# A two-layer transformer on one core: products with the values for four heads at once, in every second step

## The reference

```
h = layernorm(x) * (1 + ca) + sa;  x = x + ga * attention(h)
h = layernorm(x) * (1 + cb) + sb;  x = x + gb * experts(h)
```

```
scores = q @ k.T * 8 ** -0.5;  p = exp(scores - max);  out = (p @ v) / sum(p)
```

## Time and profile before

| | us |
|---|---|
| median of three runs | 1835.53 |
| lowest and highest | 1829.68 and 1887.89 |
| the profiled execution | 1856.04 |
| its span, first to last instruction | 1854.3 |
| first to last scores of the dense attention | 78.4 to 531.8 |
| first to last scores of the causal attention | 818.0 to 1447.2 |

### The profile page before, as it was taken

One profiled execution on the slowest core, in us unless ns is written; L12 is line 12 of the kernel. 1 busy time (PEld: TensorE's weight loads), 2 busy tenths in 40 slices (PEclk: granted clock), 3 DMA queues, 4 the chain that ended last, 5 costly groups with the idle time before them and its releaser, 6 DMA issues.

```text
span 1854.3 us, 40002 instructions
## 1 busy us (share of the span) xinstructions
PE 1575.2 (85%) x12803; PEld 808.0 (44%) x12803; DVE 1279.0 (69%) x3451; ACT 1192.9 (64%) x2134; POOL 885.1 (48%) x1677
## 2 busy tenths in 40 slices
PE   5799999999967999789999999999998409988870
PEld 3333444444433444234444444444444307777650
DVE  6565777776747888836767676666767537776657
ACT  3776777877756989635555655655645607888760
POOL 6243554545511333424443447657465654555445
PEclk9898999999988999879999998999989659999995
DMA  5221222121208920121212122222222322222218
GB/s 152 80 38 24 45 37 36 41 41 36 46 14 334 386 109 1 46 44 41 49 41 47 36 44 69 57 47 65 46 52 42 122 98 70 77 72 75 67 55 264
DMA packets 238478, 141.21 MB, mean 76 GB/s; under 512 B 184162, under 2 KB 210658, under 8 KB 237252
## 3 DMA queue, kind: packets, MB, share of 16 engines
q1 hardware_dynamic: 227072, 119.72, 24.4%
q0 software_dynamic: 8640, 17.97, 3.0%
q10 hardware_dynamic: 2564, 0.97, 0.2%
HBM read 37.67 MB, written 58.98 MB: 52 GB/s over the span
## 4 chain that ended last, share of the span: by engine, by line
PE 41%; DVE 13%; issue 6%; DVEq 2%; ACT 2%; POOL 2%; POOLq 1%; DMA 1%; SPq 0%; ACTq 0%; another core or an unknown queue 0%
PE OP L2136 8%; PE OP L2001 5%; PE M L2099 4%; PE SP L1981 4%; DVE mx L1326 4%; PE SP L2296 4%; PE M L2074 2%; PE SP L2116 2%; PE M L2095 2%; PE M L2090 2%; DVE pt L1617 2%; POOL h_dram L492 2%; PE OP L2311 2%; PE OP L2148 1%; PE M L1991 1%
## 5 line engine op out<-in xcount | busy, mean ns | idle before, releaser
L863 ACT ACTIVATE pt<-SP 128x768 f32<-128x768 f32 x256 | 207.4, 810 | 257.8 <-PE SP L2116 245.7
L1326 DVE TENSOR_REDUCE mx<-M 128x2 f32<-128x512 f32 (+1 forms) x384 | 257.9, 683 | 111.6 <-PE M L2099 103.7
L531 POOL TENSOR_SCALAR_AFFINE_SELECT pt<-pt 128x256 f32<-128x256 f32 x512 | 200.0, 415 | 273.4 <-ACT pt L863 271.7
L750 ACT ACTIVATE pt<-SP 128x1024 f32<-128x1024 f32 x256 | 255.8, 1020 | 80.4 <-PE SP L1871 80.3
L562 POOL DMA_INDIRECT y_dram<-hT,dest x142 | 138.3, 974 | 146.3 <-DVE hT L1623 123.7
L961 ACT ACTIVATE pt<-SP,b 128x256 f16<-128x256 f32 x284 | 137.4, 484 | 88.9 <-PE SP L2296 86.6
L1890 PE MATMUL OP<-pt,vs 128*32 128x256 f32 x1408 | 189.0, 391 | 0.0
L1617 DVE TENSOR_TENSOR pt<-vs,pt 128x256 f16<-128x256 f32 x284 | 117.1, 423 | 70.2 <-ACT vs L962 49.4
L2136 PE MATMUL OP<-pt,vs 128*32 128x128 f32 (+1 forms) x1408 | 156.0, 345 | 5.1 <-POOL pt L531 5.1
L492 POOL DMA_INDIRECT h_dram<-hT,slot x128 | 130.5, 1020 | 57.7 <-issue 31.6
L2296 PE MATMUL SP<-ksT,shared 128*128 128x256 f16 x852 | 130.0, 276 | 31.3 <-DVE ksT L1592 28.3
(11 more groups left out here) (325 smaller groups left out, 3362.2 us busy)
## 6 DMA issues: line engine op xcount, KB each, us to landing
h_dram<-shared SPq DMA_DIRECT2D x8, 4488.0 KB, 33.5
hT<-h_dram SPq DMA_DIRECT2D x71, 132.0 KB
rows<-g_dram SPq DMA_DIRECT2D x4, 2048.0 KB, 7.1
pt<-y_dram SPq DMA_DIRECT2D x32, 256.0 KB, 3.5
x_sb<-in_x SPq DMA_DIRECT2D x8, 512.0 KB, 8.8
pt<-in_w SPq DMA_DIRECT2D x4, 1024.0 KB
out<-x_sb SPq DMA_DIRECT2D x16, 256.0 KB, 3.0
shared<-st SPq DMA_TRANSPOSE x144, 2.4
```

The source lines that it names most:

```text
L531: last = pool.affine_select(out=diag, in_=diag, compare_op=ALU.is_ge, fill=0.0, base=0, pattern=[[0, 2], [1, P]], channel_multiplier=-1)
L750: act.activation(pt[:, u % 4], SP[u % 2][:], ACT.Exp, scale=SCALE).then_inc(s["exp"], 1)
L863: act.activation(pt[:, u % 4, :, 0:384], SP[u % 2][:, :, 0:384], ACT.Exp, scale=SCALE).then_inc(s["exp"], 1)
L1326: dve.tensor_reduce(to, M[:, k % 2, :].rearrange("p (j k) -> p j k", j=4 if k < 4 else 2), AX.X, ALU.max).then_inc(s["mred"], 1)
```

## The change

In both attentions `values` takes a group of four heads, j, in place of a step of two: for each half of the keys it issues the matmuls of all four heads, on the four column groups of the array, and then adds 2 to `pv`. It is called only in steps with odd u, for the group that ended in the step two before the last (u = 1: group 3 of the batch before; u = 3, 5, 7: groups 0, 1, 2), and waits for both steps' exponentials (dense) or selections (causal). The number of matmuls and their sizes stay.

The other work is moved. Dense: the projection of the first half of the tokens goes to step 0, that of the second half to step 2 (both were in step 1); `turn` goes from step 5 to 6. Causal: `values` now comes last in its step, behind the projections, `tail_wo`, all three fills, `router` and `back`; `enter` and `turn3` go from step 6 to 7. No other engine's list changes.

```diff
-                def values(b, u):
-
-                    if u == 0:
+                def values(b, j):
+
+                    if j == 0:
                         pe.wait_ge(s["vs"], b + 1)
-                    pe.wait_ge(s["exp"], CH * b + u + 1)
-                    if b and u % 4 == 0:
-                        pe.wait_ge(s["o"], 2 * b + u // 4 - 1)
-                        if u:
+                    pe.wait_ge(s["exp"], CH * b + 2 * j + 2)
+                    if b and j % 2 == 0:
+                        pe.wait_ge(s["o"], 2 * b + j // 2 - 1)
+                        if j:
                             pe.wait_ge(s["wr"], b)
-                    j = u // 2
+                    c = (j % 2) * T
                     for k in range(TT):
-                        for i in range(2):
-                            g = 2 * (u % 2) + i
-                            c = (j % 2) * T
+                        for g in range(HG):
                             last = pe.matmul(OP[32 * g:32 * g + 32, j // 2, c:c + T],
                                              vsd[b % 3][:, k, HG * j + g, :],
-                                             pt[:, u % 4, i, k * T:k * T + T],
+                                             pt[:, 2 * (j % 2) + g // 2, g % 2, k * T:k * T + T],
                                              start=(k == 0), stop=(k == TT - 1),
                                              skip_group_check=True, tile_position=(0, 32 * g))
-                    last.then_inc(s["pv"], 1)
+                    last.then_inc(s["pv"], 2)
...
                         score(b, u)
                         if b == 0 and u == 2:
                             pe.wait_ge(gl_in, 1)
-                        if CH * b + u >= 2:
-                            values((CH * b + u - 2) // CH, (u - 2) % CH)
-                        if u == 1 and b + 3 < B:
-                            for t in range(TT):
-                                project(b + 3, t)
+                        if u % 2 and CH * b + u >= 3:
+                            values((CH * b + u - 3) // CH, (u - 3) % CH // 2)
+                        if u in (0, 2) and b + 3 < B:
+                            project(b + 3, u // 2)
                         if u == 4 and b:
                             tail_wo(b - 1)
-                        if u == 5 and b >= 3:
+                        if u == 6 and b >= 3:
                             turn(b - 3)
                         if u == 7 and b >= 3:
                             router(b - 3)
-                values(B - 1, CH - 2)
-                values(B - 1, CH - 1)
+                values(B - 1, NJ - 1)
```

In `causal`, `values` is changed in the same way (it waits for `sel`), and the order is:

```diff
                         score(b, u)
-                        if FILLS[u] and b + 1 < B:
-                            fill(b + 1, done)
-                            done += 1
-                        if CH * b + u >= 2:
-                            values((CH * b + u - 2) // CH, (u - 2) % CH)
                         if u == 0 and b + 2 < B:
                             project(b + 2, 0)
                             project(b + 2, 1)
                         if u == 4 and b:
                             tail_wo(b - 1)
-                        for _ in range(FILLS[u] - 1):
+                        for _ in range(FILLS[u]):
                             if b + 1 < B:
                                 if done == 2 and b in WARM:
                                     keep_warm(b, u + 1, WARM[b])
...
                         if u == 5 and b >= 6:
                             router(b - 6)
                             back(b - 6)
-                        if u == 6:
+                        if u == 7:
                             if b + 3 < B:
                                 enter(b + 3)
                             if b >= 5:
                                 turn3(b - 5)
+                        if u % 2 and CH * b + u >= 3:
+                            values((CH * b + u - 3) // CH, (u - 3) % CH // 2)
                         if u == 7 and b - 1 in CHOSEN:
                             positions(CHOSEN.index(b - 1))
-                values(B - 1, CH - 2)
-                values(B - 1, CH - 1)
+                values(B - 1, NJ - 1)
```

More of the change, by code:

```diff
@@ L2119, in score, with values @@
                     last.then_inc(s["score"], 1)
-                def values(b, u):
-                    if u == 0:
+                def values(b, j):
+                    if j == 0:
                         pe.wait_ge(s["vs"], b + 1)
[L2125 to L2128, removed]
+                    pe.wait_ge(s["sel"], CH * b + 2 * j + 2)
+                    if b and j % 2 == 0:
+                        pe.wait_ge(s["o"], 2 * b + j // 2 - 1)
+                        if j:
                             pe.wait_ge(s["wr"], b)
-                    j = u // 2
+                    c = (j % 2) * T
                     for k in range(TT):
                         q0 = P if k else 0
-                        for i in range(2):
-                            g = 2 * (u % 2) + i
-                            c = (j % 2) * T
+                        for g in range(HG):
                             last = pe.matmul(OP[32 * g:32 * g + 32, j // 2, c + q0:c + T],
                                              vs3[b % 3][:, k, HG * j + g, :],
-                                             pt[:, u % 4, i, k * T:k * T + T - q0],
+                                             pt[:, 2 * (j % 2) + g // 2, g % 2, k * T:k * T + T - q0],
                                              start=(k == 0), stop=(k == TT - 1),
                                              skip_group_check=True, tile_position=(0, 32 * g))
-                    last.then_inc(s["pv"], 1)
+                    last.then_inc(s["pv"], 2)
                 def tail_wo(b):
```

## The result

The changed kernel takes 2000.74 us (median of 6, 1980.28 to 2015.32), the kernel before 1841.47 beside it (6 runs, 1829.68 to 1890.31): a ratio of 1.082, 95% interval 1.0766 to 1.0874. Every ratio here is taken over a kernel's runs without the few that fell into a slower state, so it is not the quotient of the two medians. The changed kernel is 161 us slower than predicted and outside the predicted range. The profiled execution took 2002.92 us, with a span of 2001.2.

The account below looks back on a forecast made before the run. It took TensorE and a loop through ScalarE to bind dense together, with VectorE's maxima holding up causal blocks. Dense -4, causal -18 and clock +25 gave +3 us; against the 1835.5 median it said 1840, range 1790 to 1905.

Parts of the forecast that it names:

- The clock: Causal block steps: half clock in about every second batch, some 5 us long, ended by the next four-head group; costs 25 us.
- rival C: Both attentions: half-clock stretches in every second batch last 14 us or more; 1895 us, slower, chance 0.15.
- The waits that I walked: Dense batch: scores 5 wait for exp 3, TensorE idles nearly 2 us there, and `turn` still finds z not made.
- rival E: Whole kernel: TensorE is the only bound and the walked waits mostly vanish; 1725 us, dense batch 11 us, chance 0.12.
- The saving of 0.15 us a batch: Dense loop through `high`: the stretch after the router shortens from 2.62 to 2.48 us; 4 us over 28 batches.
- The sum to 14.41: Dense batch: durations along the loop through ScalarE add up to exactly 14.41 us, read as that loop binding beside TensorE.
- Four column groups: `values`: four heads run side by side, so a group costs what two did, 0.99 us dense and 0.77 causal.
- rival D: `values`: four column groups don't run side by side, never more than two; 1897 us, slower, chance 0.10.
- The estimate of 1.15 us: Dense `values` group: cost by the skill's 3.07x for four row tiles, which would make the sum some 20 us more.
- Causal walk: Causal batch walked step by step with its waits: 18.55 us against 19.19, saving 18 us over 28 batches.
- The batch of 18.5: Causal: the batch length expected where the clock is full, against 19.19 us before.
- Rival B: Both attentions: no new half-clock stretches, so only the savings of 22 to 24 us remain; 1812 us, chance 0.18.

Follow-up runs that it names:

- e1: Changed kernel plus matmuls that nobody reads, 12 per dense batch and 9 per causal batch: 1902.22 us, ratio 1.0265 to the kernel before.
- e10: Changed kernel with each four-head group's products issued as two pairs, one after the other: 2029.64 us, ratio 1.0995 to the kernel before.
- e7: Kernel before with four heads at once in dense alone, old places, plus 8 and 8 unread matmuls ahead of `tail_wo` and `turn`: 1784.15 us, ratio 0.9879.
- e12: Kernel before with four heads at once in dense alone, old places, plus 4 and 4 unread matmuls ahead of `tail_wo` and `turn`: 1825.57 us, ratio 0.9884.
- e5: Changed kernel's new places in both attentions, but products of two heads in every step as in the kernel before: 1920.12 us, ratio 1.0358.
- e13: Changed kernel with TensorE waiting for a group's first pair of heads before issuing the second: 2044.24 us, ratio 1.1298 to the kernel before.
- e6: Kernel before with four heads at once in dense alone, everything else in its old place: 1785.8 us, ratio 0.9872.
- e4: Changed kernel with four heads at once kept in both attentions, but all other work back in its old place: 1947.95 us, ratio 1.0555.
- e9: Kernel before plus 9 unread 512-column matmuls per causal batch in steps 2 to 4: 1847.76 us, ratio 1.022.
- e8: Kernel before with four heads at once in causal alone, old places, plus three unread 512-column matmuls in steps 2 and 4: 1825.22 us, ratio 1.009.

## Why the prediction was wrong

**The clock, the step that failed.** I put it at 28 batches x 0.5 x 5 us x 0.35 = 25 us in causal, and at nothing in dense. The place was right: the clock falls in the block steps of the causal batch (1116.0, in step 3, between the seventh block and the eighth). How often was wrong by a factor of two: every batch, not every second. How long was wrong by three: 491 us over 31 stretches is 15.8 each, as the two that I had in front of me were 13.7 and 17.1. I set those rows aside for an argument, that the dense group that follows would bring the clock back; nothing in the trace stood for it, and the group at 1118.40 shows the opposite. The price was near: with 19.0 us for a full-clock batch (e1), (737 - 31 x 19.0) / 491 = 0.30 us lost per us at half, and single batches of the change (24.0 us, 17 of them at half) give 0.29. So the term was 31 x 15.8 x 0.30 = 147 us in causal, not 25; the stage is longer by only 124, because the kernel before had lost some 11 us at half too and its full-clock batches are longer (19.2). This is rival C with its own length taken in every batch, which I gave 0.15 and priced at half.

**Dense.** The waits that I walked came: TensorE idles 1.8 to 2.0 us before scores 5 ("nearly 2"), and rival E's 11 us did not come. The saving of 0.15 us a batch was too small. The change's shortest batches, with 3 us at half clock in them, take 13.4 and 13.6, and e10's one batch without any takes 13.4, against 13.9 on average before (most 13.7 to 14.4); in the old places (e7, e12) it is 13.0. The sum to 14.41 could not show that ScalarE's loop binds: it adds up the distances from one place in the batch to the same place in the next, which gives the batch by whatever path. This error put the forecast too high; what put it too low is that I wrote that idle time down as free. It is what the clock answered to: 215 us at half, and 22 us more for the stage instead of 4 less. In the trace the falls in dense come with the longest waits (252.4 behind 1.79 us, 450.4 with 1.96), and where filler took the waits away the falls went too (e7: 3 stretches, 14 us). Those in causal do not: TensorE was busy 6.47 of the 6.9 us that ended at 1116.0. The Trainium skill, page "TensorE: Matmul & The Clock Gate", section "Part 1: The HAM clock gate", ties a fall to idle gaps; dense agrees in kind, causal is nearer to what the same page says under "A second HAM failure mode: psum-queue depth-cycling", that short idle times between groups of matmuls can make the clock swing too. No run here tests that against the thin work of the blocks themselves.

**Four column groups.** Right, and rival D is out: sixteen matmuls take 1.00 us (301.53 to 302.53 after), starting in fours within 20 ns, and 0.79 in causal. The timeline after:

```profile
301.53 1.07 PE L1888 MATMUL OP<-pt,shared 128*32 128x256 f32 x16
302.53 0.39 PE L1871 MATMUL SP<-shared 32*128 32x256 f16 x4
```

The estimate of 1.15 us that I drew from the Trainium skill's four row tiles does not carry over to four column tiles.

**Causal walk.** Its waits came: 0.25 and 0.61 us for the blocks, 0.86 for `turn3` (0.8 predicted), this one at half clock. The batch of 18.5 was never seen, because the change has no batch at full clock; e1's 19.0 has 1.9 us of filler in it, so it does not refute the walk. What the order is worth with the clock held for nothing stays open.

**Rival B** is out (51 stretches). (The chances for "slower" add up to 0.30, not 0.29.) **The moves** I had costed at nothing or hidden; alone they cost 1.0 us in a full-clock causal batch (e5), and on top of the merge 0.4 us in a full-clock dense batch (13.4 in e10 against 13.0 in e7) and 37 us of the stage in all.

**What is shown and what is not.** Shown: the loss is time at half clock for the most part (e1 gives some 100 us back with added work), it is 1.010 in dense and 1.070 in causal, and in dense it comes from the shorter products (e13) by the idle time that they leave (e7). The merge pays in dense in the old places (e6), where TensorE waits for ScalarE. Not shown: why a causal stretch at half clock lasts longer than a dense one, and what in the causal block steps makes the clock fall; e4 says that the moves are not needed for it, e13 points to the short products not being needed either, but it adds waits of its own and is not a pure test.

## What to carry to other kernels

A change that makes TensorE's work shorter without shortening the loop around it leaves idle time, and that time has a price: look up what the clock did after idle or thin stretches in the trace of before, and charge that length to every place that the change thins out (here 31 causal batches x 15.8 us x 0.30). Two long stretches at half clock in a trace are better evidence on their length than a mechanism thought up for why the next will be short. Merge where another engine sets the pace, leave the rest of the order alone, and look at the granted clock before counting saved matmul time.

## What the runs showed of the hardware

- TensorE at 91% busy (900 to 1560 after) has a granted clock of 0.67, at 86% (140 to 540) of 0.77, and e6 at 79% of 0.87. With filler e7 is at 86% too, and its clock is 1.00, so the share alone does not tell. A high busy share can itself come of a low clock: at half a group of four heads is busy 1.93 us, not 1.07.
- Matmuls that nobody reads made a kernel faster by some 100 us (e1), and cost 1.3 us a batch where the clock was full anyway (e9).
- Once filler held the clock in one thin place of the loop, the falls moved to the next: to `turn` in dense (e1), to `turn3` in causal (e8).
- Issuing the products of four heads as two pairs, one after the other, did not part them: four matmuls started within 34 ns, and the group took no longer (e10), so TensorE must have started some of the second pair with the first, although they stand behind it in its list. To keep them apart took a wait for the first pair (e13).
